# Scatter-adds of successive groups without a wait between them, group transposes in two banks, and a row load moved ahead of two stores

## The reference

```python
route_prob = jax.nn.softmax(xt @ Ws + bs, axis=-1)
p = jnp.max(route_prob, axis=-1)
routes = jnp.argmax(route_prob, axis=-1)
h = jax.nn.gelu(jnp.einsum('td,edf->tef', xt, W1) + b1, approximate=False)
out = jnp.einsum('tef,efd->ted', h, W2) + b2
common = out[:, 0, :]
sel = jnp.take_along_axis(out, routes[:, None, None], axis=1)[:, 0, :]
scaling = (p / jax.lax.stop_gradient(p))[:, None]
pe = p[:, None]
final = jnp.where((routes == 0)[:, None], common * scaling, pe * sel + (1.0 - pe) * common)
```

## Time and profile before

| | us |
|---|---|
| median of 3 runs (390.5 to 396.18) | 390.6 |
| the profiled execution's own time | 390.53 |
| its span, first to last instruction | 388.7 |
| PE busy in the span | 365.3 (94%) |
| POOL busy in the span | 188.7 (49%) |

### The profile page before, as it was taken

The page is one execution under the profiler, slowest core; times in us unless marked ns, Lnnn a source line. Parts: engine busy times, 40 slices in busy tenths (PEclk is TensorE's granted clock), DMA queues, the critical chain, the costliest instruction groups (busy, mean ns, idle before and its releaser), DMA issues.

```text
span 388.7 us, 10470 instructions
## 1 busy us (share of the span) xinstructions
PE 365.3 (94%) x3291; PEld 326.7 (84%) x3292; DVE 172.6 (44%) x595; ACT 164.0 (42%) x553; POOL 188.7 (49%) x307
## 2 busy tenths in 40 slices
PE   7899999999999999899999999998999999999980
PEld 6677877888888888788888999987999999999980
DVE  3365766778777797444222363412111111221110
ACT  0122133233333353778443543335445554554430
POOL 1667977777777786542012007720333333334433
PEclk9999999999999999999999999999999999999996
DMA  8664335353311345335002607445665666676510
GB/s 250 229 204 113 106 98 170 97 166 97 89 50 46 127 140 163 96 97 203 2 0 82 177 0 226 150 88 164 170 164 153 167 156 158 177 179 170 161 15 0
DMA packets 40589, 49.58 MB, mean 128 GB/s; under 512 B 10412, under 2 KB 32313, under 8 KB 40553
## 3 DMA queue, kind: packets, MB, share of 16 engines
q1 hardware_dynamic: 34641, 42.95, 37.0%
q0 software_dynamic: 5024, 5.72, 7.4%
q10 hardware_dynamic: 888, 0.45, 0.4%
HBM read 39.84 MB, written 10.27 MB: 129 GB/s over the span
## 4 chain that ended last, share of the span: by engine, by line
PE 52%; DMA 23%; issue 8%; POOL 3%; DVE 2%; POOLq 1%; ACT 1%; SPq 0%; DVEq 0%; ACTq 0%
DMA out<-ARENA,ID 21%; PE bank L504 7%; PE score_banks L575 7%; PE bank L637 7%; PE score_banks L619 5%; PE bank L592 5%; PE bank L535 3%; POOL packed_tokens L1353 3%; PE score_banks L627 3%; PE bank L536 2%; PE bank L558 2%; PE bank L610 2%; PE bank L545 1%; PE bank L611 1%; PE bank L546 1%
## 5 line engine op out<-in xcount | busy, mean ns | idle before, releaser
L637 PE MATMUL bank<-W,ARENA 128*128 (+1 forms) x516 | 94.6, 334 | 1.5 <-issue 1.2
L637 PEld LDWEIGHTS bank<-W,ARENA 128*128 128x128 f32 x516 | 82.8, 190 | 5.7 <-issue 1.5
L1369 POOL DMA_INDIRECT out<-ARENA,ID x25 | 39.4, 1575 | 75.0 <-DMA out<-ARENA,ID 62.5
L851 ACT ACTIVATE ARENA<-score_banks,B1R 128x128 f32<-128x128 f32 x150 | 41.5, 376 | 39.5 <-PE score_banks L627 36.4
L851 ACT ACTIVATE ARENA<-score_banks,B1T 128x128 f32<-128x128 f32 x108 | 29.9, 375 | 31.8 <-PE score_banks L627 31.8
L1265 POOL TENSOR_TENSOR VS<-V,R 108x384 f32<-108x384 f32 x32 | 27.7, 867 | 30.5 <-DVE R L956 30.1
L1228 DVE TENSOR_TENSOR ARENA<-bank,B 128x192 f32<-128x192 f32 x25 | 9.0, 358 | 72.7 <-PE bank L637 70.4
L619 PE MATMUL score_banks<-RINGS,W1R 128*128 128x128 f32 x300 | 37.6, 275 | 0.0
L1256 POOL TENSOR_TENSOR RINGS<-QK,GM 128x216 f32<-128x216 f32 x64 | 34.3, 556 | 3.4 <-PE score_banks L575 3.4
L619 PEld LDWEIGHTS score_banks<-RINGS,W1R 128*128 128x128 f32 x300 | 35.5, 192 | 0.1
L575 PEld LDWEIGHTS score_banks<-QK,RINGS 48*108 48x108 f32 x512 | 28.7, 171 | 6.1 <-issue 2.9
(11 more groups left out here) (149 smaller groups left out, 623.2 us busy)
## 6 DMA issues: line engine op xcount, KB each, us to landing
W1R<-in_w SPq DMA_DIRECT2D x25, 384.0 KB
V<-v_rows SPq DMA_DIRECT2D x96, 54.0 KB
W<-in_w SPq DMA_DIRECT2D x9, 576.0 KB, 4.2
W1R<-in_w_rest SPq DMA_DIRECT2D x50, 96.0 KB
ARENA<-in_patches SPq DMA_DIRECT2D x11, 384.0 KB, 3.5
packed_tokens<-RINGS POOLq DMA_DIRECT2D x1, 2425.0 KB, 12.1
ARENA<-packed_tokens SPq DMA_DIRECT2D x25, 97.0 KB, 2.5
PT<-in_patches SPq DMA_DIRECT2D x6, 384.0 KB, 3.3
```

Of the source, the lines that this page charges most:

```text
L637: last = pe.matmul(bank[2 * par][:, 0:D], HT[par][:, c * P:c * P + P], W2[:, bass.ds((expert * FC + c) * D, D)], start=c == 0, stop=c == F ...
L851: last = act.activation(HT[par][:, to:to + P], bank[6 + g][:, c * P:c * P + P], ACT.Gelu, bias=b1[:, bias:bias + 1])
L1369: pool.indirect_dma_start(out, bass.IndirectOffsetOnAxis(ap=ID[par][:, 0:1], axis=0), YR[par], None, bounds_check=TOKENS - 1, oob_is_err=F ...
```

## The change

Three edits. POOL's wait L1367 is removed: a scatter-add is held only by its own number copy, its own scaled rows, and the scatter-add two groups back. The transposes of even groups go to `bank[4]`, those of odd groups to `bank[5]`; transposes of group n wait for ACT's copy of group n-2, and the first two for none. On SP the row load of group 2 is issued after the stores of base tiles 12 to 15 and before those of tiles 16 and 17, which now stand inside `load_group` between the row load of group 2 and the wait L475.

```diff
--- before.py
+++ after.py
@@ -60,6 +60,7 @@
 ROW_PARTS = ((0, 2), (2, 8), (8, TILES))
 STEPS = IMAGES // STEP_IMAGES
 BASES_FIRST = 12
+BASES_SECOND = 16
 
 
 PAIR_STEPS = STEPS // 2
@@ -465,13 +466,16 @@
                 sp.dma_start(XF[r], packed[r * P:r * P + P]).then_inc(xr_in[r], 16)
             sp.dma_start(SLOT_ROWS[:, :].rearrange("p (g w) -> p g w", w=2),
                          packed.rearrange("(g p) w -> p g w", p=P)[:, :, D:ROW]).then_inc(slot_rows_in, 16)
-            for t in range(BASES_FIRST, TILES):
+            for t in range(BASES_FIRST, BASES_SECOND):
                 store_base(t)
 
             def load_group(i, ks):
                 n, par, half = tile_at(i, ks[0])
                 sp.wait_ge(ffn_t_done, n - 1)
                 sp.dma_start(XF[par], packed[bass.ds(n * P, P)]).then_inc(xr_in[par], 16)
+                if ks[0] == 2:
+                    for t in range(BASES_SECOND, TILES):
+                        store_base(t)
                 sp.wait_ge(f1_done, 2 * (TILES + n - 1))
                 load_group_up(n, par)
 
@@ -666,9 +670,9 @@
             def transpose_group(i, k):
                 n, par, half = tile_at(i, k)
                 pe.wait_ge(xr_in[par], 16 * (half + 1))
-                if k >= 1:
-                    pe.wait_ge(ffn_xt, n)
-                transpose_tile(XF[par], bank[5]).then_inc(ffn_t_done, 1)
+                if k >= 2:
+                    pe.wait_ge(ffn_xt, n - 1)
+                transpose_tile(XF[par], bank[4 + par]).then_inc(ffn_t_done, 1)
 
             def transpose_xn2(t):
                 pe.wait_ge(xn2_ready, t + 1)
@@ -886,7 +890,7 @@
 
             def copy_group(n, par):
                 act.wait_ge(ffn_t_done, n + 1)
-                copy_twice(XTF[par], bank[5]).then_inc(ffn_xt, 1)
+                copy_twice(XTF[par], bank[4 + par]).then_inc(ffn_xt, 1)
 
             def group_step(i, ks):
                 kx, kg = ks
@@ -1363,8 +1367,6 @@
                 pool.tensor_copy(ID[par][:, :], SLOT_ROWS[:, bass.ds(2 * n + 1, 1)].bitcast(I32)).then_inc(id_ready, 1)
                 pool.wait_ge(id_ready, n + 1)
                 pool.wait_ge(y_scaled, n + 1)
-                if kh >= 1:
-                    pool.wait_ge(y_added[1 - par], 16 * (half + par))
                 ride(pool)
                 pool.indirect_dma_start(out, bass.IndirectOffsetOnAxis(ap=ID[par][:, 0:1], axis=0), YR[par], None,
                                         bounds_check=TOKENS - 1, oob_is_err=False,
```

## The result

The six executions of the changed kernel have a median of 394.3 us (386.88 to 400.15), those of the kernel before beside them 392.61 us (390.5 to 396.18). Three of the six took 400.0 to 400.2 us, with a mean granted clock of TensorE of 0.956 instead of 0.993, because the clock fell to its lower level (1.2 GHz) for some 31 us of the attention stage, long before the first changed instruction; it does so in executions of the kernel before too (up to 405.9 us), and the comparison leaves such executions out. It gives a ratio of 0.9891, with a 95% interval of 0.9847 to 0.9935: the changed kernel is faster by 1.1%, some 4.3 us, which is less than the 2% that would count as faster. The profiled execution took 386.88 us where 386.4 was predicted; the median of all six lies outside the range of 384.7 to 388.3.

The account below looks back on a forecast made before the run. PE alone was taken to set the pace mid-stage, so gains come only at the group stage's ends: 390.53 - 1.07 - 3.11 = 386.35, given as 386.4 us against the runs' median; range 384.7 to 388.3.

Parts of the forecast that it names:

- the sum: Whole kernel: profiled execution of 390.53 us less 1.07 at the start of the group stage and 3.11 at its end, 386.35.
- The tail: End of the group stage: without POOL's wait L1367 the last scatter-add starts at 380.12 instead of 383.23, 3.11 us gained.
- POOL's pace: End of the group stage: scatter-add, number copy, next scatter-add take 2.67 us, which sets when the last scatter-add starts.
- The start: Start of the group stage: transposes of group 2 come 1.68 us sooner, of which 1.07 us are left after group 3's rows.
- the rows of group 3: Start of the group stage: issued 0.25 us sooner, landing in 2.6 us, they make PE wait again, about 0.6 us.
- the second bank: Start of the group stage: PE's up products of group 0 begin 0.25 us sooner; in the loop it gives nothing.
- The weights of group 2: Start of the group stage: needed only after the transposes, so no later bound than the rows of group 3.
- The first, a lost start: Start of the group stage: rows of group 2 or 3 land late, only 0.3 or 0.1 us gained; 387.3 us, chance 0.16.
- The second, that both ends give all: Both ends of the group stage: full gains of 1.68 and 3.81 us; 385.1 us, chance 0.14.
- The third, scatter-adds that serialize: End of the group stage: scatter-adds queue behind each other; 386.5 us, or 387.2 with long landings, those at chance 0.06.
- The fourth, collisions with the row loads: Group loop: scatter-adds disturb row loads, PE waits in every group; at 4.0 us landings 391.9 us, slower; chance 0.05.

## Why the prediction was right or wrong

**The range.** Here a step failed: the range was drawn from the terms of the sum alone, around a profiled execution of 390.53 us, and the clock in the attention stage was put at nothing without a reason, although 396.18 us stood among the three times of before. Measured, it costs some 13 us (400.0 against 386.9) in three of the six executions, and it alone puts the median outside the range: 390.6 x 0.9891 is 386.3 us, where the sum put 386.4. That these two agree so closely is luck, for the interval of the ratio is 3.4 us wide and the trace shows 3.78 us gained, not the 4.18 of the sum. Why the clock falls in one execution and not in another stays open. So does whether the change has a part in it: over 399 us were 7 of 14 executions of the changed kernel, 10 of 48 of the kernel before, and 10 of 42 of the four other kernels that were timed repeatedly.

**What bounds the kernel.** Right: the loop has the same step before and after, 4.574 us, and from the first up product of group 2 to its last product PE takes 106.88 us in both; the removed wait was worth nothing there, and in the change as a whole it made 3.12 of 3.78 us.

**The tail.** Right in mechanism and size. POOL's pace sets the last scatter-add, not the scaling: 2.67 us from the scatter-add of group 23 to that of group 24 (376.90 to 379.57), as summed, and 3.12 us gained where 3.11 were predicted. The part that was assumed, 0.87 us from the end of the copy to the next scatter-add, is 0.90. The experiment with the copies made ahead shows that this pace held the end: without it the last scatter-add follows its scaled rows by 0.86 us.

**The start.** The sum put 1.07 us, the trace has 0.66. The step that failed here is the one from "the transposes of group 2 start at 264.26" straight to the rows of group 3. The row load of group 2 did move as worked out: it was issued 1.63 us after the common down products instead of 3.26, and the transposes of group 2 start 3.77 us after them instead of 5.34, 1.57 us sooner where 1.68 were predicted. But between these and the rows of group 3 lies a wait that the prediction did not look at: the up products of group 1 use the PSUM banks 6 and 7, and wait until ACT's gelu has read those of group 0 out of them. Before, PE stood still for the row load at that time and the gelu was done behind it; with the row load early it comes out, 0.57 us. When the up products of group 1 begin (4.78 us after the common down products, before 5.62), only 0.84 of the 1.57 us are left. In the loop the down products of another group lie in between and hide this wait.

The rows of group 3 were next in line as predicted, but their size was wrong too. They were issued 6.46 us after the common down products, before 6.52: 0.06 sooner, not 0.25, since the second bank saved only 0.13 us (the first up products came 1.22 instead of 1.35 us after the common down products). They landed 2.76 us after their issue, not 2.6, at 269.94 in the trace, and the transposes that need them began at 269.98, just as the products ahead of them ended. So the gelu and the rows came out at the same time, and either alone holds the start near 9.5 us: 9.67 with the gelu wait taken away, 9.46 with the rows made early. That a new wait of about 0.6 us did appear, as predicted for the rows, is chance: it is the gelu's. The weights of group 2, said to be no later bound, landed 0.49 us before PE came to them.

**The rivals.** The first, a lost start, is the nearest: a part of the start was lost, to the gelu and, at the same time, to the rows of group 3. The second, that both ends give all, did not come about. The third, scatter-adds that serialize, can't be told from POOL's pace in the changed kernel, where that of group 24 is issued at 379.57 and that of group 23 lands at 379.63. In the kernel with the copies made ahead it falls: the scatter-add of group 24 is issued 0.74 us before that of group 23 has landed, and lands 2.69 us after its issue, where the last one before took 2.72. The fourth, collisions with the row loads, did not come about: the row loads land in 2.1 to 3.4 us, 2.8 in the median, 0.2 longer than in the earlier trace rows, and PE still has no wait in the loop. The rule of the page "DMA: Bandwidth & Descriptors" of the Trainium skill, section "Issuing engines are not separate DMA queues", that all queues share the engines, is not contradicted by the longer median; here it cost nothing.

## What to carry to other kernels

A wait that fills the waiting engine's idle time is worth nothing as long as another engine sets the pace; it is worth its backlog at the end, where the engine that set the pace has stopped. It could be taken away here because each token goes to one picked expert, so that no two groups add to the same row of `out`. When a stall is taken away, look for every other wait of the same instruction stream up to the next steady step, also those the trace reports with nothing, for the stall was what hid them: here the gelu and the next rows came out together, with the weights close behind, and each edit uncovered another. And a time that is to lie within a range of 1% needs the spread of the runs in the range, not only the terms of the sum.

## What the runs showed of the hardware

A scatter-add of 128 rows on POOL can start while the one before it is on its way: with nothing between them two started 1.97 us apart, the distance at which their rows were scaled, and landed 2.71 and 2.69 us after their issue, so they were on their way together for 0.74 us. With the number copy between them they start 2.67 us apart. From the start of the last one to the end of the span it took 5.45 to 5.47 us in each of the nine kernels.

One and the same program had, in one execution, a stretch of 31 us at a granted clock of 0.50 that began in a 1.4 us pause of PE, and in another none at the same pause; in traces of other kernels here the stretch lasted 3 us or 14 us.
